# Selective-scan stage: matrix B's parts laid on 128 partitions, and another split of the sixteen B products among ScalarE, VectorE and GpSimd

## What is computed

```python
dt, Bm, Cm = split(xc @ x_w.T, [4, 20])     # xc: 128 channels, Bm and Cm: 16 states each
dt  = softplus(dt @ dt_w.T + dt_b)
dA  = exp(dt[..., None] * A)                # channel x state
dBx = dt[..., None] * Bm[:, :, None, :] * xc[..., None]
h   = dA_t * h + dBx_t                      # the scan over t
y   = sum over states of h * C_t            # then + xc * D, * silu(z), @ out_w.T
```

## Time and profile before

| | |
|---|---|
| median of three runs | 2651.32 us (2651.02 to 2654.09) |
| the profiled execution | 2649.26 us, of which the span of its records is 2647.5 us |
| scan, forward part | 738 to 1578 us of the span, about 52.8 us a chunk |
| scan, backward part | 1578 to 2441 us of the span, about 54 us a chunk |
| busy share of the span | PE 87%, DVE 82%, POOL 78%, ACT 67% |

### The profile page before, as it was taken

How to read it: one execution, slowest core, us unless ns; L and a number is a source line. 1 busy time by engine, 2 the same in 40 slices (tenths; PEclk the granted TensorE clock), 3 DMA queues, 4 the chain that set the end, 5 groups by cost and what they waited for, 6 DMA issues and landing times. The chain is left out here.

```text
span 2647.5 us, 37695 instructions
## 1 busy us (share of the span) xinstructions
PE 2314.0 (87%) x9340; PEld 1130.1 (43%) x9340; DVE 2157.9 (82%) x2101; ACT 1779.2 (67%) x4094; POOL 2073.5 (78%) x1327
## 2 busy tenths in 40 slices
PE   7899998585599999999999999899999999998597
PEld 6566666243344444434444433333333333333543
DVE  4566666605399999999999999999999999998866
ACT  4788888435587778877877766556565566653376
POOL 4455555301399999999999999999999999998389
PEclk7899999696799999999999999999999999999799
DMA  4000000001466666666677777767777777764032
GB/s 68 13 12 10 12 10 9 2 0 23 121 216 225 227 225 228 225 223 228 225 224 227 228 240 253 237 230 242 235 240 231 240 245 236 237 219 168 3 66 62
DMA packets 186406, 421.05 MB, mean 159 GB/s; under 512 B 66548, under 2 KB 87513, under 8 KB 186330
## 3 DMA queue, kind: packets, MB, share of 16 engines
q1 hardware_dynamic: 184794, 416.01, 49.4%
q10 hardware_dynamic: 1536, 4.20, 0.5%
HBM read 387.63 MB, written 24.12 MB: 156 GB/s over the span
## 5 line engine op out<-in xcount | busy, mean ns | idle before, releaser
L1549 POOL TENSOR_TENSOR s_hc<-s_h,s_cc 128x1024 f32<-128x1024 f32 x512 | 1200.7, 2361 | 63.0 <-PE s_py L1312 45.6
L1312 PE MATMUL s_py<-s_hc,ident 128*128 128x512 f32 x2048 | 1018.7, 623 | 8.7 <-DVE s_yo L1594 8.7
L1631 DVE TENSOR_TENSOR_SCAN s_h<-s_dA,s_state,s_pu 128x1024 f32<-128x1024 f32 x330 | 770.5, 2342 | 29.6 <-PE s_pu L1290 6.1
L1312 PEld LDWEIGHTS s_py<-s_hc,ident 128*128 128x128 f32 x2048 | 364.1, 193 | 455.8 <-issue 425.0
L1465 ACT ACTIVATE s_dA<-s_dt,ss_A 128x1024 f32<-128x1024 f32 x352 | 401.8, 1143 | 9.2 <-ACT s_brow L1428 7.7
L1470 ACT ACTIVATE s_pu<-s_dt,ss_A 128x1024 f32<-128x1024 f32 x160 | 178.6, 1116 | 319.7 <-DVE s_h L1631 314.6
L1542 POOL TENSOR_TENSOR s_dbx<-s_dtx,s_bb 128x1024 f32<-128x1024 f32 x160 | 377.7, 2361 | 7.1 <-DMA s_bb<-rows_scratch 7.1
L1607 DVE TENSOR_TENSOR s_pu<-s_pu,s_dtx 128x1024 f32<-128x1024 f32 x288 | 349.8, 1215 | 25.3 <-PE s_pu L1299 25.3
L1631 DVE TENSOR_TENSOR_SCAN s_h<-s_pu,s_state,s_dbx 128x1024 f32<-128x1024 f32 x150 | 350.3, 2335 | 15.6 <-ACT s_pu L1470 14.6
L581 POOL TENSOR_TENSOR ar_ex<-ar_ex,ar_rs 128x512 f32<-128x512 f32 x128 | 133.0, 1039 | 190.6 <-DVE ar_rs L536 190.6
L1299 PE MATMUL s_pu<-s_bcs,ss_sel 48*128 48x512 bf16 x576 | 174.8, 384 | 92.1 <-DVE s_h L1631 92.0
(11 more groups left out here) (269 smaller groups left out, 3702.3 us busy)
## 6 DMA issues: line engine op xcount, KB each, us to landing
s_cc<-rows_scratch SPq DMA_DIRECT2D x512, 512.0 KB, 4.6
s_bb<-rows_scratch SPq DMA_DIRECT2D x160, 512.0 KB, 4.9
s_n<-n_scratch SPq DMA_DIRECT2D x64, 258.0 KB, 5.6
y_scratch<-s_yo SPq DMA_DIRECT2D x16, 512.0 KB, 5.3
s_yf<-y_scratch SPq DMA_DIRECT2D x16, 512.0 KB, 6.6
x_tok<-in_x_dram SPq DMA_DIRECT2D x16, 256.0 KB, 4.6
at_xg<-at_xT SPq DMA_DIRECT2D x64, 64.0 KB, 2.1
n_scratch<-ss_turned SPq DMA_DIRECT2D x32, 128.0 KB, 2.3
```

Of the source, the lines that this page charges most:

```text
L1312: ins = nc.tensor.matmul(p_y[:, hf], lhsT=c.ident[:, :], rhs=hc[:, s % RING, hf], start=(s == 0), stop=(s == U - 1))
L1549: nc.gpsimd.tensor_tensor(hc[:, s % RING, :], h[:, s % RING, :], cc[:, s % C_RING, :], ALU.mult).then_inc(read, 1)
L1631: nc.vector.tensor_tensor_scan(out=flow(h[:, s % RING, :]), data0=flow(decays), data1=flow(inputs), initial=begun, op0=ALU.mult, op1=ALU.a ...
```

## The change

Three things. The tile `bcs` and the matrix `sel` are made 128 partitions high; partitions 48 to 127 are set to zero once at the start of the scan (a memset on POOL, for which DVE and SP wait), and `spread_b` multiplies all 128 rows. The forward states become V V G A V A V A G V A V A G A V from 0 (7 V, 6 A, 3 G); the backward ones stay. Since the number of G states is now odd, two helpers count the landings and the uses of the two `bb` slots; and since 13 forward states now have their decay in SBUF, the ring of decays has five slots forward and not four.

```diff
-BY_VECTOR = ((0, 1, 4, 7, 8, 11, 13, 15),
+BY_VECTOR = ((0, 1, 4, 6, 9, 11, 15),
              (0, 1, 3, 4, 6, 8, 9, 11, 12, 14))
-BY_SCALAR = ((3, 5, 9, 12), ())
+BY_SCALAR = ((3, 5, 7, 10, 12, 14), ())
...
-            sel=sb("ss_sel", [3 * STATES, STATES], BF16))
+            sel=sb("ss_sel", [128, STATES], BF16))
...
+    def landed(self, n, r):
+
+        w, slot = self.of(n), r % B_RING
+        per = len(w.g[slot::B_RING])
+        done = NC * len(w.before.g[slot::B_RING]) if w.before is not None else 0
+        return n * per + (done - w.start * per) + r // B_RING + 1
+
+    def row_used(self, n, r):
+
+        w, first = self.of(n), self.upto(lambda v: v.g, n)
+        if r >= B_RING:
+            return first + r - B_RING + 1
+        last = [q for q in range(len(w.g)) if q % B_RING == r][-1]
+        return first - len(w.g) + last + 1
...
-        bcs = sb("bcs", [3 * STATES, 2, TC], BF16)
+        bcs = sb("bcs", [128, 2, TC], BF16)
...
-                                           lhsT=k["sel"][:, s:s + 1].to_broadcast([3 * STATES, 128]),
+                                           lhsT=k["sel"][:, s:s + 1].to_broadcast([128, 128]),
...
-                pool.wait_ge(b_spread[r % B_RING], 16 * (w.upto(G, n, B_RING) + r // B_RING + 1))
+                pool.wait_ge(b_spread[r % B_RING], 16 * w.landed(n, r))
...
+            nc.gpsimd.memset(bcs[:, :, :], 0.0).then_inc(zeroed, 1)
...
-            dve.wait_ge(zeroed, 1)
+            dve.wait_ge(zeroed, 2)
...
-                need(sp, g_injected, w.upto(G, n) + r + 1 - B_RING)
+                need(sp, g_injected, w.row_used(n, r))
...
-                sp.dma_start(bcs[:, m % 2, :],
+                sp.dma_start(bcs[0:3 * STATES, m % 2, :],
...
             load_n(1)
+            sp.wait_ge(zeroed, 2)
             load_flat(0)
```

## The result

The changed kernel took 2719.4 us (median of four runs, 2712.4 to 2724.6) against 2651.5 before: a ratio of 1.0254, 95% interval 1.0221 to 1.0287, so 68 us slower. The forecast was 2708 in a range of 2672 to 2760. The profiled execution took 2724.0 us, with a span of 2722.3; it is one of the two slower of the four (the others took 2724.6, 2714.7 and 2712.4). The numbers of the lines have moved: the scan is now L1647, DVE's product L1623, its `lost` L1590; ACT's two decays are L1480 and L1485, its `scale` L1463, `bc_rows` L1443, relu L1414, `softplus_one` L1427; PE's spread is L1314, turn L1305, total L1327, `columns_b` L1288.

A forecast was written before the change was run, and what follows sets the result against it. Forward chunks were taken as set by DVE plus about 3.2 us waiting for ACT and PE, backward by POOL. 60 - 1 - 4.5 - 2 + 4.5 = +57 us on 2649.3 led to a median of 2708, range 2672 to 2760.

The forecast's parts named there:

- parts 1 and 2: Forward chunk: DVE loses one product (1.12 us), POOL one (2.36); ACT gains two scales, about 4.9 us.
- Part 2 and 3, the first delay: Forward units 4 to 6: `bc_rows` ends 3.4 us later, holding `columns_b` and a spread; scan 6 starts at 20.6, not 15.1.
- part 6: Forward PE after the new wait before `columns_b`: lower clock costs 0.3 us a chunk, +4.5 us, between 0 and 22.
- Part 4, the second delay: Forward ACT queue from scan 6 to `softplus_one`: `lost` starts at 33.1, DVE ready at some 31.3; chunks +4.0 on average.
- the one sign that I named: Forward DVE: a new idle group before `lost`, waiting for ACT, of 1 to 2 us a chunk.
- Part 5, the rows: PE's spreads on 128 rows load weights ahead: -0.3 us a forward chunk, -4.5 us, at most -9; backward -2.
- The balance wins: Rival: `bc_rows` arrives before PE is ready, forward chunks lose 1.1 to 1.3 us; 2627 us, chance 0.14.
- Half of it: Rival: the forward wait before `lost` does not come, 27 us less; 2681 us, chance 0.14.
- The clock takes over: Rival: after each stall PE runs at 1.2 GHz, delaying totals and `step_size` before relu; 50 more, 2758 us, chance 0.08.

The follow-up runs named there:

- e3: The changed kernel with ACT's forward `bc_rows` moved to the end of unit 3, ahead of the scale of state 7; 2669.6 us, ratio 1.0062.
- e4: The changed kernel with PE's forward `columns_b` moved to unit 5, behind the spread of state 6; 2664.1 us, ratio 1.0049.
- e6: The changed kernel with PE repeating the spread of state 6 seven times while it waits for `bc_rows`; 2705.5 us, ratio 1.0201.
- e7: e3 with state 10 made by VectorE and not by ScalarE; 2654.7 us, ratio 1.0000.
- e1: The changed kernel with the old order of states, so the 128 partitions alone; 2637.2 us, ratio 0.9946.
- e2: The changed kernel with 48 rows again, so the new order of states alone; 2735.9 us, ratio 1.0324.
- e8: e1 with one more product by ScalarE, at state 7; 2721.3 us, ratio 1.0257.
- after_again: The changed kernel, unaltered, run once more for a second trace; 2717.9 us.
- e5: e1 with one more product by ScalarE, at state 13; 2632.0 us, ratio 0.9927.

## Why the prediction was right, step by step

**What bounds the kernel (parts 1 and 2): right.** DVE and POOL lost their work (743 to 723, 745 to 710 us busy in the forward part) and it bought nothing.

**Part 2 and 3, the first delay: right in mechanism and place.** `bc_rows` ended at 16.4 where I had 16.6. Scan 6 ended at 24.0 (1255.35 + 2.35, less 1233.71) where I had 22.95; what is more is PE's clock (part 6). e3 and e4 remove this delay from its two sides, on ACT and on PE, and each brings the chunk to 53 to 54.

**Part 4, the second delay: right on ACT, but mostly hidden.** From scan 6's end to `lost` the trace has 10.1 us (1257.70 to 1267.77) and I had 10.2; from `lost` to the next chunk's start 22.9 (1290.71) and I had 23.0. But I had DVE ready for `lost` 1.8 us ahead of that, and it was not: in this chunk it waited 0.8 us for the turn of state 7 and 1.0 for the spread of state 9, and ended scan 9 just as ACT ended `softplus_one`. So the wait itself showed as 6 us in all and not 15 to 30, the one sign that I named and that did not come. The time is as forecast there only because ACT and DVE were late together. With PE's slow stretch away (e3, e6) the wait came to light, 28.1 and 26.3 us; in e7 it went away.

**Part 6, the clock: the term that was mis-sized.** I took 0.3 us a chunk in the chain. In the chunk shown the chain carried 2.79 less 1.80 for `columns_b` and 0.81 less 0.43 for the spread, 1.4 us; net of the second delay, e6 gives at least 0.6 a chunk, 9 us and not 4.5. It was within the 22 us that I kept as a bound.

**Part 5, the rows: a little too small.** I took two thirds of 0.3 us; the whole was there. Forward it gave 6.6 us (e1 against before) and 7.9 (the changed kernel against e2), where I had 4.5; backward 2.2 and nothing, where I had 2.

**Counting the chunks.** Fourteen of the fifteen intervals have the stall; they grew from 52.8 to 57.3 us on average (802.7 over 14), +4.5 and not +4.0. The last, without `columns_b`, took 48.9 and not the 51.5 that I had, 2.9 below before. Its second delay, which I had kept, was there as 1.4 us; where the other 2.6 us of this miss lie is not worked out. The first stall lies before the first `take_y`, where the trace shows +1.0 and I had +4: that chunk, from its first scan to that of the next, grew from 53.7 to 56.1 us (57.8 in the second trace), but its first scan had started 2.3 us earlier. Together 14 x 4.5 - 2.9 + 1.0 = 61, where my parts 1 to 6 gave 59 forward. That the sum hit so closely is in part luck: 7 us too little for the fourteen chunks, and 2 and 3 us too much for the last and the first, cancel.

**The rivals.** "The balance wins" fell at the point that I named: slack before `columns_b` under 0.5 us. "Half of it" did not come as a time, though its condition did: the wait before `lost` was 0.4 us a chunk. DVE was late for another reason. "The clock takes over" did not decide here, but e8 shows that it can: there the slow PE stood before relu.

**Not forecast:** the 13 us behind the scan, seen in the one trace and, by their times, in two of the four runs (last section). The median lies midway between the two pairs, so it takes in about half of them, 7 of the 11 us between +57 and the +68 of the medians. The other 4 are small misses: 2 forward, 1.2 at the change of direction, 0.7 backward.

## What to carry to other kernels

Ask of work that is moved to an engine with room where in its queue it lands and who waits behind that place: the same 2.35 us of ACT cost 4.3 us a chunk ahead of a copy that PE needed, and gained 1.0 us behind it. Follow the late signal one queue further: PE had next to nothing to do for DVE behind `columns_b` before, and a spread row after. And before costing two delays as a sum, see whether one hides the other, as here the clock and the softplus did.

## What the runs showed of the hardware that I had not expected

**Row count and loading ahead.** A 48-row bf16 weight load between 128-row ones began only with its matmul, and so did the next one; with 128 rows both were loaded 0.2 to 0.4 us ahead. That is 0.3 us a pair of matmuls, and 13 to 14 us of the kernel by the medians of e1, 9 of which its trace shows in the scan.

**Stalls of 2.0 to 2.4 us, and the clock behind them.** In the changed kernel the granted clock fell to 0.50 behind each of the 14 stalls before `columns_b` (2.30 to 2.38 us idle), and in e8 behind 13 of 14 (1.95 to 2.31). In the chunk shown it was 0.73 over 1250 to 1252, 0.50 until 1256, 0.57 over 1256 to 1258 and 1.00 after that: low for nearly 7 us, with PE busy throughout. The length of the idle time alone does not say whether it falls: in e8 it stayed at 1.00 behind 2.30 us once, and behind 1.25 us at 1225.97.

**A clock that stays low although PE is full.** Behind the scan, in the experts' normalisation, PE does transposes of 128 x 128 and matmuls of 16 columns. Windows of the kernel before, of the changed kernel, and of `after_again`, in that stage:

```profile
2475.00:2485.00 10.00, 9.85 (x86) 9.65 (x87) 6.30 (x15) 5.94 (x13) 6.71 (x6) 1.00 0.01 2
```

```profile
2536.00:2546.00 10.00, 10.00 (x49) 10.00 (x48) 6.95 (x15) 4.88 (x11) 5.27 (x5) 0.50 0.00 0
```

```profile
2540.00:2550.00 10.00, 9.85 (x85) 9.53 (x83) 9.22 (x20) 7.13 (x16) 7.39 (x6) 1.00 0.01 2
```

and PE's timeline of the changed kernel just before:

```profile
2532.90 1.16 PE L252 MATMUL ex_n_ps<-ident,ex_n_out 128*128 128x128 f32 x8 [1.25 <-POOL ex_n_out L232]
2533.90 1.34 PE L1783 MATMUL er_ps<-ex_wr,ex_xT 128*128 128x16 f32 x8
2535.08 2.06 PE L252 MATMUL ex_n_ps<-ident,ex_n_out 128*128 128x128 f32 x8
```

PE was idle once for 1.25 us, fell to 1.2 GHz and, though busy for the whole of the next 20 us, did not come back before the stage was over: 49 records in 10 us and not 86 (a record is one matmul or transpose). The stretch behind the last gate is 207, 220 and 208 us in these three executions. It goes with the execution and not with the code: of the two traces of the e5 program one has 205.8 us there and the other 219.6, with the same forward part (769.8 us both). The four runs of the changed kernel fall into 2712 to 2715 and 2724 to 2725, which fits this; for the runs without a trace that is inferred, and `after_again` with its 2717.9 lies between the pairs. Over all fourteen traces of this case the stretch is 218 to 221 us in seven and 205 to 208 in the other seven. In the seven long ones PE was idle for 1.2 to 1.3 us some 30 us behind the gate, and the clock was at 0.50 from a few us later to the end of the stage; in the seven short ones the idle time there was at most 1.05 us or there was none, and the clock stayed at 1.00. That the idle time is what brings the clock down is not shown by this, and why its length differs between executions was not tried.
